# A four-layer Fourier convolution tower: convolution as 32x32 taps on a halo that holds each pixel once

## The reference, cut to what matters

```python
h = concat([grid, x], -1) @ P_w + P_b            # 5 -> 32 channels, NCHW after
for i in range(4):
    h_ft = rfft2(h)
    modes = einsum('bixy,ioxy->boxy', h_ft[:, :, :16, :16], spec_wr[i] + 1j * spec_wi[i])
    spec = irfft2(modes, s=(64, 64))
    conv = conv3x3(h, conv_w[i], 'SAME') + conv_b[i]
    h = leaky(spec + conv)                       # leaky: slope 0.01
h = leaky(h @ Q1_w + Q1_b)                       # 32 -> 32
out = (h @ Q2_w + Q2_b)[..., 0]                  # 32 -> 1
```

## Time and profile before

| | us |
|---|---|
| runs | 1377.09, 1379.96, 1383.61; median 1379.96 |
| profiled execution | 1379.42, span on the core 1377.6 |
| mean granted TensorE clock | 0.951 of full |
| PE busy | 1248.0 |
| PEld busy | 709.5 |
| DVE busy | 541.0 |
| ACT busy | 493.1 |

### The profile page before, as it was taken

How to read it: one execution, slowest core, us unless ns; L and a number is a source line. 1 busy time by engine, 2 the same in 40 slices (tenths; PEclk the granted TensorE clock), 3 DMA queues, 4 the chain that set the end, 5 groups by cost and what they waited for, 6 DMA issues and landing times. The chain is left out here.

```text
span 1377.6 us, 42277 instructions
## 1 busy us (share of the span) xinstructions
PE 1248.0 (91%) x19664; PEld 709.5 (52%) x19664; DVE 541.0 (39%) x553; ACT 493.1 (36%) x934; POOL 66.8 (5%) x122
## 2 busy tenths in 40 slices
PE   4899997999999998999999989999999943799955
PEld 2566664555555555545555554434444413489945
DVE  3656753333353334333353322110111104667785
ACT  1255654033333332233333333334444432425511
POOL 2000000000000000000000000011111110000000
PEclk9999998999999999999999999999999976979967
DMA  8354547667666776766666663556655407000000
GB/s 279 140 158 132 147 159 190 217 192 190 191 190 191 191 190 219 191 190 191 190 192 193 191 187 74 121 130 129 129 121 116 89 3 157 0 1 1 1 0 16
DMA packets 39359, 192.53 MB, mean 140 GB/s; under 512 B 16432, under 2 KB 16560, under 8 KB 17456
## 3 DMA queue, kind: packets, MB, share of 16 engines
q1 hardware_dynamic: 30224, 137.39, 40.3%
q0 software_dynamic: 8960, 52.44, 10.5%
HBM read 136.84 MB, written 52.95 MB: 138 GB/s over the span
## 5 line engine op out<-in xcount | busy, mean ns | idle before, releaser
L376 PE MATMUL psum<-halo,conv 128*64 128x512 f32 x2304 | 516.2, 598 | 2.8 <-DMA halo<-activations 2.6
L504 ACT ACTIVATE x_now<-psum,conv_bias 128x512 f32<-128x512 f32 x256 | 172.9, 688 | 525.4 <-PE psum L387 508.1
L376 PEld LDWEIGHTS psum<-halo,conv 128*64 128x64 f32 x2304 | 157.5, 136 | 322.0 <-issue 318.6
L574 DVE STREAM_TRANSPOSE ft<-psum 128x1024 f32<-128x1024 f32 x50 | 98.3, 1966 | 380.3 <-PE psum L290 380.3
L387 PE MATMUL psum<-dft,vt 128*32 128x128 f32 x8192 | 241.0, 273 | 0.7 <-issue 0.6
L387 PEld LDWEIGHTS psum<-dft,vt 128*32 128x32 f32 x8192 | 220.7, 110 | 39.0 <-issue 39.0
L597 DVE STREAM_TRANSPOSE vt<-psum 128x1024 f32<-128x1024 f32 x64 | 126.0, 1969 | 249.3 <-PE psum L352 249.3
L487 ACT ACTIVATE spec<-psum 32x128 f32<-32x128 f32 x384 | 147.2, 383 | 40.3 <-PE psum L303 36.4
L567 DVE STREAM_TRANSPOSE xt<-x_now 128x1024 f32<-128x1024 f32 x100 | 124.0, 1242 | 34.0 <-ACT x_now L504 28.2
L352 PE MATMUL psum<-zt,dft 64*32 64x256 f32 x2048 | 78.2, 380 | 5.4 <-DVE zt L590 5.4
L511 ACT ACTIVATE xt<-psum,q1b 128x512 f32<-128x512 f32 x64 | 40.5, 683 | 106.8 <-PE psum L401 106.8
(11 more groups left out here) (133 smaller groups left out, 776.5 us busy)
## 6 DMA issues: line engine op xcount, KB each, us to landing
activations<-x_now POOLq DMA_DIRECT2D x48, 1056.0 KB, 8.7
halo<-activations SPq DMA_DIRECT2D x192, 264.0 KB, 7.4
halo<-activations SPq DMA_DIRECT2D x192, 263.9 KB, 7.6
wspec<-in_spec SPq DMA_DIRECT2D x16, 1024.0 KB, 9.6
xcol<-in_xcol SPq DMA_DIRECT2D x16, 384.0 KB, 4.5
x_now<-in_ser SPq DMA_DIRECT2D x2, 1056.0 KB, 6.7
t_lq<-in_onehot SPq DMA_DIRECT2D x1, 2048.0 KB, 14.8
t_kr<-in_causal SPq DMA_DIRECT2D x1, 2048.0 KB, 24.9
```

Source lines behind the costliest of these rows:

```text
L376: mm(acc[u][64 * r:64 * r + 64, :], conv[:, l - 1, dy, :], rows[:, at:at + 16, 0:G], start=(dy == 0), stop=False, skip_group_check=True)
L504: copy(x_now[:, k, 16 * u:16 * u + 16, 0:G], acc[u].rearrange("p (i j) -> p i j", j=G), ACT.Prelu, bias=conv_bias[:, l:l + 1], alpha=SLOPE ...
L574: vec.transpose(ft[:].rearrange("p k c -> p c k"), rowed.rearrange("p a b -> p (a b)").rearrange("p (i c) -> p c i", c=C)).then_inc(s_ft, 1)
```

## The change

- The halo holds each pixel once, in the partitions in which x_now has it, with two rows of zeros above and below. Its load is one DMA for layer 1. For layers 2 and 3 it is 16 DMAs of 32 partitions by one unit (66 KB), because the four phases of unit u of a tile are now written to partition groups XORed with u (`turn`), and the load undoes this. A load waits for the accumulators of T-2 only where an earlier tile's convolution has used the buffer.
- `convolve` becomes `taps(T, d)`. Output phase and input phase differ by d (0 to 3: bit 1 for row parity, bit 0 for column parity); for each tap of this d, for each u and for each input phase f there is one matmul of 32 partitions by 32 outputs, 512 pixels wide. In all it is 9 taps x 4 units x 4 phases = 144 calls instead of 24. Within one tap the 16 calls use 16 different 32x32 tiles of the array: unit u and phase f write partition group f ^ d ^ u of bank u.
- Each stage d waits for the whole stage before it (s_seg; the first for all four evictions of the tile before, s_x, and for the halo).
- The order in a pair becomes: taps 3, rows_forward, columns_back, taps 1, spectral 0, taps 2, spectral 1, taps 0, spectral 2, spectral 3, columns_forward. In the last layer: taps 3, head_hidden, taps 1, head_hidden, taps 2, head_out, spectral 0 and 1, taps 0, spectral 2 and 3, columns_back. For p = 0 columns_back comes after the spectral blocks. Between layers: taps 3, rows_forward, taps 1, columns_forward, wait, mix, columns_back, taps 2, taps 0.
- rows_forward goes in two halves of 256 columns (one per unit parity), 16 calls instead of 8. Layer 0 keeps its convolution and its order.
- head_out writes 32 partitions per unit, so that `head_read` is one activation of 128 partitions, placed before evict 0.

```diff
+        def turn(l, u):
+            return u if l > 0 else 0
...
-                reached(sp, s_acc, 4 * (T - 2) + 4)
...
+                if src >= 2:
+                    sp.wait_ge(s_acc, 4 * (T - 2) + 4)
+                if l == 1:
+                    sp.dma_start(halo[:, k, TOP:TOP + PLANE], x_d[p]).then_inc(s_halo[k], 16)
+                    return
+                for u in range(4):
+                    for f in range(4):
+                        g = 32 * (f ^ turn(l - 1, u))
+                        sp.dma_start(halo[32 * f:32 * f + 32, k, TOP + UNIT * u:TOP + UNIT * u + UNIT],
+                                     x_d[p, g:g + 32, UNIT * u:UNIT * u + UNIT]).then_inc(s_halo[k], 16)
...
-                for dy in range(3):
-                    for r in range(2):
-                        y = r + dy - 1
-                        at = 16 * u + (2 * (y // 2) + (2 * G + 2 if y % 2 else 0))
-                        mm(acc[u][64 * r:64 * r + 64, :], conv[:, l - 1, dy, :], rows[:, at:at + 16, 0:G],
-                           start=(dy == 0), stop=False, skip_group_check=True)
+            def taps(T, d):
...
+                if d == 3:
+                    pe.wait_ge(s_x, 4 * T)
+                    pe.wait_ge(s_halo[k], halo_loads(T))
+                else:
+                    pe.wait_ge(s_seg, 3 * (T - PAIRS) + {1: 1, 2: 2, 0: 3}[d])
+                for dy in ((-1, 1) if d & 2 else (0,)):
+                    for dx in ((-1, 1) if d & 1 else (0,)):
+                        w = 3 * (dy + 1) + dx + 1
+                        for u in range(4):
+                            for f in range(4):
+                                to, r, s = f ^ d ^ u, (f ^ d) // 2, (f ^ d) % 2
+                                di, dj = (r + dy - f // 2) // 2, (s + dx - f % 2) // 2
+                                at = TOP + (16 * u + 2 * di) * PITCH + dj
+                                rows = halo[32 * f:32 * f + 32, k, at:at + UNIT].rearrange("p (i j) -> p i j", j=PITCH)
+                                z = mm(acc[u][32 * to:32 * to + 32, :], conv[32 * f:32 * f + 32, l - 1, w, :],
+                                       rows[:, :, 0:G], start=(d == 3 and dy == -1 and dx == -1), stop=False,
+                                       skip_group_check=True)
+                if d > 0:
+                    z.then_inc(s_seg, 1)
+                elif p > 0:
+                    z.then_inc(s_acc, 2)
...
+                taps(T, 3)
+                rows_forward(T + 1)
+                if p < LAST:
+                    columns_back(T + 1)
+                taps(T, 1)
+                spectral(T, 0)
+                taps(T, 2)
+                spectral(T, 1)
+                taps(T, 0)
+                spectral(T, 2)
+                spectral(T, 3)
+                columns_forward(T + 1)
...
-                for u in range(4):
-                    z = copy(h_now[32 * u:32 * u + 4, k, :], valued[32 * u:32 * u + 4, :], ACT.Identity,
-                             bias=q2b[32 * u:32 * u + 4, :])
-                z.then_inc(s_h, 1)
+                copy(h_now[:, k, :], valued, ACT.Identity, bias=q2b[:]).then_inc(s_h, 1)
```

More of the change, by code:

```diff
@@ L408, in head_out, with first_pair @@
                 for u in range(4):
-                    z = mm(valued[32 * u:32 * u + 4, :], q2w[:, u % 2, :], hid[:, u, :], start=True, stop=True)
+                    z = mm(valued[32 * u:32 * u + 32, :], q2w[:, u // 2, :], hid[:, u, :], start=True, stop=True)
                 z.then_inc(s_y, 1)
-            def pair(l, p, last):
+            def first_pair(p):
+                T = p
+                if p > 0:
+                    convolve_first(T)
+                    rows_forward(T + 1)
+                    if p < LAST:
+                        columns_back(T + 1)
+                for u in range(4):
+                    spectral(T, u)
+                if p > 0:
+                    columns_forward(T + 1)
+                else:
+                    columns_back(T + 1)
@@ L414, in pair @@
+            def pair(l, p):
                 T = l * PAIRS + p
-                if p > 0:
+                if p == 0:
                     for u in range(4):
-                        convolve(T, u)
-                        if last and u % 2 == 0:
-                            head_hidden(p - 1, u)
-                    if not last:
-                        rows_forward(T + 1)
+                        spectral(T, u)
+                    columns_back(T + 1)
+                    return
+                taps(T, 3)
+                rows_forward(T + 1)
@@ L422, in pair @@
                 if p < LAST:
                     columns_back(T + 1)
-                for u in range(4):
-                    spectral(T, u)
-                    if last and p > 0 and u == 0:
-                        head_out(p - 1)
-                if p > 0 and not last:
-                    columns_forward(T + 1)
+                taps(T, 1)
[5 more added lines that the diff above has]
+                spectral(T, 3)
@@ new lines, in pair, with last_pair @@
+                columns_forward(T + 1)
+            def last_pair(p):
+                T = (NL - 1) * PAIRS + p
+                if p == 0:
+                    for u in range(4):
+                        spectral(T, u)
+                    columns_back(T + 1)
+                    return
+                taps(T, 3)
+                head_hidden(p - 1, 0)
+                taps(T, 1)
+                head_hidden(p - 1, 2)
+                taps(T, 2)
+                head_out(p - 1)
+                spectral(T, 0)
+                spectral(T, 1)
+                taps(T, 0)
+                spectral(T, 2)
+                spectral(T, 3)
+                if p < LAST:
+                    columns_back(T + 1)
@@ L431, in _, with boundary @@
+            def boundary(l):
+                T = l * PAIRS
+                taps(T, 3)
+                rows_forward(T + 1)
+                taps(T, 1)
+                columns_forward(T + 1)
+                pe.wait_ge(s_spec, T + 2)
+                mix(l)
+                columns_back(T)
+                taps(T, 2)
+                taps(T, 0)
             pe.wait_ge(s_const, 16 * 4)
@@ L444, in _ @@
             columns_back(0)
[L445 to L446 removed]
+            convolve_first(0)
             for p in range(PAIRS):
[L448 removed]
+                first_pair(p)
             for l in range(1, NL):
[L450 to L459 removed]
+                boundary(l)
                 for p in range(PAIRS):
[L461 removed]
+                    if l == NL - 1:
+                        last_pair(p)
+                    else:
+                        pair(l, p)
             head_hidden(LAST, 0)
@@ L541, in _ @@
                         head_activate(p - 1, u)
-                evict(T, 0)
-                if last and p > 0:
                     head_read(p - 1)
-                for u in range(1, 4):
+                for u in range(4):
                     evict(T, u)
```

120 lines of the change are left out of this document (49 added, 71 removed).

## The result

The changed kernel takes 1425.04 us in the median (1423.14 to 1426.73), the kernel before, on the same chip, 1380.16 (1377.09 to 1383.61). The ratio is 1.032, 95% interval 1.030 to 1.035: 45 us slower, where 36 us faster was forecast. The profiled execution took 1424.67 us, span 1422.9. All medians here are of undisturbed executions; two far slower ones, 2730 us of b1_before_no_traffic and 6328 us of e10_fine_and_late, are left out.

What follows compares the result with a forecast made beforehand. It took the order and density of PE's own instructions as the bound in layers 1 and 2; terms -6.0, -13.7, -6.4, -4.5, -2.4 and -2.8 sum to -35.8, taking 1379.4 to 1343.6 us, range 1290 to 1383.

Steps and rivals of the forecast that it cites:

- the rivals: Other outcomes: unlimited tiles 1295 us (0.22); evictions showing 1366 us (0.12); half the tiles 1630 us or late halo (together 0.14).
- DMA. ... Cost 0: Layers 2 and 3: 16 halo DMAs a tile take 6.8 to 15.0 us, needed after 19.8; cost 0, 4.8 us left.
- Convolution as taps, -6.0 us: 30 full pairs of layers 1 and 2: 9 rounds instead of 12, 16.86 us a pair, -0.20 each, -6.0 us.
- fast rival: Tap rounds: nothing limits the 16 tiles, a later round takes 0.86 us, taps(3) 3.7; 1295 us in all, chance 0.22.
- the slow one: Tap rounds: only 8 tiles run together, 1.72 us a round, taps(3) 7; 1630 us, chance 0.14 shared with late halo.
- reading of the queue: In front of PE: 64 instructions in flight, each leaving 0.61 us after its pass begins; later tap rounds take 1.05 us.
- Evictions hidden "by a hair": Wait for s_x after taps(0): ACT's fourth eviction done after about 2.8 us, PE busy 2.86, so no cost.
- Last layer, -13.7: 15 last-layer pairs: taps and head_hidden as one stretch of one shape, 17.42 us a pair, -0.91 each, -13.7 us.
- First boundary, -6.4: First layer boundary: halo wait, the convolution's slowness and half of the mix's slowness go, -6.4 us.
- Boundaries, -4.5: Three layer boundaries: taps(2) and taps(0) take 3.5 instead of 5.3 us, taps(3) delays the spectrum 0.3; -1.5 each, -4.5.
- first pairs, -2.4: First full pair of each layer: the 0.8 us lost while evictions run goes, as columns_back stands there; -2.4 us.
- The end, -2.8: Kernel's end: head_read 2.06 us shorter on the path and evictions no longer queued behind it, -2.8 us.

Runs made afterwards that it cites:

- b1_before_no_traffic: Kernel before, with halo loads of 16 columns and stores of 17 in place of 2112, all instructions and waits kept; 1372.0 us, ratio 0.988-0.996.
- e10_fine_and_late: e3 plus the next layer's spectral weights in 32 DMAs of 128 KB behind the halo loads of pairs 2 to 7; 1362.4 us, ratio 0.978-0.990.
- e2_no_traffic: Changed kernel with halo loads and stores moving 16 columns in place of 2112, all compute instructions and waits kept; 1357.4 us, ratio 0.977-0.986.
- e7: Changed kernel with layer 1's halo in 16 DMAs of 66 KB and the store in four quarters; 1364.5 us, ratio 0.977-0.989.
- e3: Changed kernel with layer 1's halo in 16 DMAs, store in four quarters, halo load held until the pair's first tap group ran; 1361.9 us, ratio 0.980-0.990.

## Why the prediction was wrong

The mechanism that decided was not among the rivals. Step by step:

- **The step that failed: "DMA. ... Cost 0"**, and with it what the taps cost beside their rounds. It asked of the new DMAs only whether the halo comes in time, and it does: no wait for a halo is left at any boundary. It never asked who else needs the DMA engines at that moment: TensorE's own instructions. And the taps were priced by their rounds alone: a pair has some 1090 TensorE instructions instead of 580, so its blocks last 4.36 us instead of 7.35 (medians of layer 1), and the instruction supply lost the slack that had covered late refills. The term measured: 54.8 us of stops in the three layers (7.6 without traffic, 4.6 in the kernel before) and 10.3 us of clock behind them.
- **Convolution as taps, -6.0 us.** Right per pair: 16.93 us against 16.86 forecast and 17.06 before, and taps(3) 4.40 against 4.3. The fast rival (3.7) and the slow one (7) are out: in the first round, at 727.12, all 16 passes start within 0.13 us, four row groups into each bank. The reading of the queue held: second calls of the 16 tiles start about 0.62 us behind their tile's second pass. Over 30 pairs it would be -3.9. The real means were 20.3 us in layer 1 and 17.9 in layer 2 (pairs 1 to 13).
- **Evictions hidden "by a hair".** Right: no undisturbed pair shows a wait for ACT.
- **Last layer, -13.7.** Right, and more: 17.25 us a pair against 17.42 forecast, 18.33 before; the layer is 15.1 us shorter. The timeline of the changed kernel:

```profile
1024.40 4.47 PE L398 MATMUL psum<-halo,conv 32*32 32x512 f32 x128
...
1041.65 0.81 PE L398 MATMUL psum<-halo,conv 32*32 32x512 f32 x16
```

- **First boundary, -6.4.** The wait for the halo is gone and the mix took 9.23 us instead of 10.29, but layer 0 ends at 226.52 as before: seven stops of its own, 6.3 us, took the gain (the kernel before has 6.1 us of stops there, 3.7 of them in the one just ahead of the halo wait). Without traffic it is 222.79. The term was added up wrong besides: 2.61, 2.74 and half of 2.45 are 6.6.
- **Boundaries, -4.5, and first pairs, -2.4.** Half right. taps(2) and taps(0) take 3.49 us (3.5 forecast), and the first pair begins at full pace. But from the boundary's convolution to the first pair layer 2 takes 36.15 us in e2_no_traffic, and 31.68 before: 2.56 are idle time at two block ends while the weights' 4 MB load, and 1.4 a mix of 9.24 us instead of 7.84. It is part of why e2 came out 7 to 12 us a layer above my expectation; I had taken the boundaries at their forecast length. The mix's length follows the granted clock. Windows over one mix each, three of the kernel before, then two of the changed one:

```profile
530.37:538.21 7.84, 7.84 (x256) 7.67 (x256) 3.75 (x3) 0.00 (x0) 0.00 (x0) 1.00 0.03 6
818.87:828.10 9.23, 9.23 (x256) 9.09 (x256) 3.75 (x3) 0.00 (x0) 0.00 (x0) 0.82 0.02 6
239.94:250.23 10.29, 10.29 (x256) 10.15 (x256) 3.75 (x3) 0.00 (x0) 0.00 (x0) 0.72 0.01 2
```

```profile
238.87:248.10 9.23, 9.23 (x256) 9.10 (x256) 3.75 (x3) 0.00 (x0) 0.00 (x0) 0.82 0.02 4
575.37:585.70 10.33, 10.33 (x256) 10.19 (x256) 3.75 (x3) 0.00 (x0) 0.00 (x0) 0.72 0.01 3
```

All five stand behind the same wait of 3.2 us for ACT's spectrum. Why the clock falls behind it for none, some or more of the mix stays open; that it needs no traffic is seen in e2_no_traffic (9.24 us at 0.82 in layer 2) and b1 (7.69 at 1.00, and 9.23 at 0.82 in layer 3).
- **The end, -2.8.** Right in its first part; before the last head_hidden TensorE idles 0.81 us instead of 2.12, and one head_read takes 0.69 instead of 2.75.

```profile
1162.21 1.09 PE L430 MATMUL psum<-x_now,q1w 32*32 32x512 f32 x16 [0.81 <-ACT x_now L579]
1169.94 0.69 ACT L593 ACTIVATE ft<-psum,q2b 128x512 f32<-128x512 f32 x1 [2.05 <-PE psum L438]
```

The account against the kernel before: layer 0 0, layer 1 +42.5, layer 2 +18.2, layer 3 -15.1, behind it -0.4, together the span's +45.3. With most stops away the forecast's direction holds: e2's tower ends 21 us before that of the kernel before, e7's and e3's 10.

But the 21 us flatter the change, since the kernel before gains from the same cut. Without traffic on either side (e2 against b1) the changed tower is 7.5 us shorter, 1095.5 against 1103.0: layer 3 -18.1, layers 1 and 2 +2.6 and +5.0, layer 0 +3.1. So the refills explain the loss of 45 us, and not all of the distance to the forecast. Even without the traffic only the last layer's term came in, and in the middle layers the 2 us a layer that the pairs gain are lost again at the boundaries.

## To carry to other kernels

When a change swaps few large instructions for many small ones, work out how long TensorE now takes over 256 of them, and hold that against the time in which the DMA engines may be full at one go; at 4.4 us a block, a load and a store of 1 MB issued within a microsecond of each other were enough to stop it. Bytes and mean DMA share don't show this: cut large DMAs that nobody waits for into pieces that leave apart, the store first, and look for idle time by "issue" at places that don't follow the code. A stop can be paid a second time in the clock: in layer 1 five stops of 2.3 to 3.4 us were, with 10.3 us in all.

## Not expected of the hardware

- A refill of 16 KB can stand behind large DMAs for far longer than one of their records takes: it started up to 5.7 us after the block end that called for it (the one for 324.96, with the longest stop, 3.4 us), where 0.2 to 1.1 is usual. The Trainium skill ("DMA: Bandwidth & Descriptors", Queues, rings and completion order) has each DMA engine take turns between its queues, a packet at a time. The trace could agree only if a packet is all that one DMA has on an engine: 1056 KB are 8 records of 8448 B an engine at 0.32 us, 2.6 us, and load and store together 5.1. By single records of two queues the wait would be 0.6 us. That reading also fits the 66 KB loads and the quarter stores, but no run measured it by itself, and the trace does not tell which DMA engine carried a refill.
- Each packet is called for one block ahead, and no earlier. When TensorE goes on past a block end, the latest packet to have started is the one called for at the block end before (at 239 of the 251 block ends of the changed kernel) or one more (at 12), and in none of the thirteen traces does TensorE go on less than 1.17 us after that packet's end. So there is one block in hand, some 4 us. The Trainium skill ("Runtime: NRT & Kernel Launch", Instruction fetch mechanics) gives TensorE room for 2048 instructions, which would be eight blocks and 30 us of cover here; the stops show that it had no such cover.
